# Adapter weights fetched in pieces of 512 bytes instead of 2 KB

## The reference

```
x      : (128, 32, 512) float32          ids : (128,) int32, drawn from 3..7
weight : (8, 512, 512) float32
out    = x + einsum('bsi,boi->bso', x, weight[ids])
```

## Time and profile before

| | |
|---|---|
| median of 3 runs | 113.01 us (112.57 to 115.44) |
| the profiled execution's own time | 112.28 us |
| its span, first to last instruction | 110.4 us |
| PE busy | 101.7 us, 92% |
| ACT busy, DVE busy | 56.9 us (52%), 53.4 us (48%) |
| granted TensorE clock | 1.000 throughout |
| DMA | 22.92 MB, mean 208 GB/s |

### The profile page before, as it was taken

How to read it: one execution, slowest core, us unless ns; L and a number is a source line. 1 busy time by engine, 2 the same in 40 slices (tenths; PEclk the granted TensorE clock), 3 DMA queues, 4 the chain that set the end, 5 groups by cost and what they waited for, 6 DMA issues and landing times.

```text
span 110.4 us, 2351 instructions
## 1 busy us (share of the span) xinstructions
PE 101.7 (92%) x458; PEld 81.6 (74%) x458; DVE 53.4 (48%) x107; ACT 56.9 (52%) x103; POOL 36.1 (33%) x45
## 2 busy tenths in 40 slices
PE   5399995998999999999999999999999999999960
PEld 3148883875888888888888888888888888888840
DVE  1286952794844483468663575556282222220000
ACT  3108404567932892399575749738494443442220
POOL 7200000024670257036653624531634334330000
PEclk9999999999999999999999999999999999999999
DMA  1815597898899699947776476675466564723333
GB/s 21 290 70 144 145 384 188 265 296 214 283 353 375 142 292 365 364 135 229 254 228 216 135 255 186 220 221 183 127 198 225 186 239 130 233 116 110 101 95 95
DMA packets 25598, 22.92 MB, mean 208 GB/s; under 512 B 3264, under 2 KB 20672, under 8 KB 25584
## 3 DMA queue, kind: packets, MB, share of 16 engines
q1 hardware_dynamic: 20112, 9.84, 32.2%
q0 software_dynamic: 2400, 7.54, 18.1%
q10 hardware_dynamic: 3072, 5.37, 15.8%
HBM read 17.30 MB, written 8.91 MB: 238 GB/s over the span
## 4 chain that ended last, share of the span: by engine, by line
PE 72%; DMA 7%; ACT 5%; SPq 4%; DVE 4%; issue 3%; ACTq 1%; DVEq 0%
PE out_ps L461 72%; DMA x_raw<-in_x 4%; DMA ids_i<-in_ids 3%; SPq L158 3%; ACT w_hi L283 2%; ACT xt_hi L268 2%; DVE w_raw L375 1%; SPq L152 1%; ACT out_tile L290 1%; DVE w_lo L379 1%; DVE xt_lo L384 0%; ACTq L264 0%; DVE masked L355 0%; DVE in_slot L361 0%; DVE is_own L346 0%
## 5 line engine op out<-in xcount | busy, mean ns | idle before, releaser
L461 PE MATMUL out_ps<-w_hi,xt_hi 128*128 x136 | 53.4, 393 | 1.7 <-ACT xt_hi L268 1.7
L243 POOL DMA_INDIRECT out<-out_tile,row_of x30 | 33.3, 1111 | 61.2 <-ACT out_tile L290 57.9
L461 PE MATMUL out_ps<-w_lo,xt_hi 128*128 x136 | 53.0, 390 | 0.0
L384 DVE TENSOR_TENSOR xt_lo<-x_raw,xt_hi 128x512 fp32r<-128x512 f32 x34 | 23.6, 694 | 33.8 <-ACT xt_hi L268 33.7
L461 PE MATMUL out_ps<-w_hi,xt_lo 128*128 x136 | 36.4, 389 | 0.0
L268 ACT ACTIVATE xt_hi<-x_raw 128x512 fp32r<-128x512 f32 (+1 forms) x35 | 21.5, 616 | 20.8 <-DMA x_raw<-in_x 19.6
L461 PEld LDWEIGHTS out_ps<-w_hi,xt_hi 128*128 128x128 f32 x136 | 25.5, 188 | 8.2 <-issue 3.1
L461 PEld LDWEIGHTS out_ps<-w_hi,xt_lo 128*128 128x128 f32 x136 | 25.5, 188 | 5.4
L461 PEld LDWEIGHTS out_ps<-w_lo,xt_hi 128*128 128x128 f32 x136 | 25.5, 188 | 5.1
L283 ACT ACTIVATE w_hi<-w_raw 128x512 fp32r<-128x512 f32 x32 | 19.4, 621 | 15.0 <-DVE w_raw L375 15.0
L290 ACT ACTIVATE out_tile<-out_ps 128x512 f32<-128x512 f32 x34 | 19.9, 586 | 12.8 <-PE out_ps L461 12.8
(11 more groups left out here) (50 smaller groups left out, 8.8 us busy)
## 6 DMA issues: line engine op xcount, KB each, us to landing
x_raw<-in_x SPq DMA_DIRECT2D x134, 64.0 KB, 2.1
w_raw<-in_weight ACTq DMA_DIRECT2D x7, 1024.0 KB
w_raw<-in_weight ACTq DMA_DIRECT2D x2, 256.0 KB, 4.6
w_raw<-in_weight SPq DMA_DIRECT2D x2, 256.0 KB, 5.0
out<-out_tile ACTq DMA_DIRECT2D x8, 64.0 KB, 1.8
out<-out_tile SPq DMA_DIRECT2D x8, 64.0 KB, 1.8
out<-out_tile,row_of POOLq DMA_INDIRECT x30, 3.3
x_raw<-in_x ACTq DMA_DIRECT2D x2, 64.0 KB
```

The lines of the kernel that those rows point to most:

```text
L243: nc.gpsimd.indirect_dma_start(out=out_rows, out_offset=bass.IndirectOffsetOnAxis(ap=row_of[:, t:t + 1], axis=0), in_=out_tile[n][:, :], i ...
L384: nc.vector.tensor_tensor(xt_lo[t % XT_BUFS][:, :, :, :], x_raw[t % X_BUFS][:, :, :, :].rearrange("p m c r -> p c m r"), xt_hi[t % XT_BUFS ...
L461: return nc.tensor.matmul(out_ps[n][:, :], left[k][:, c, :, :].rearrange("p m r -> p (m r)"), right[:, bass.ds(rank, 1), c, :].rearrange(" ...
```

## The change

The cap on one piece of the weight DMA of ranks 1 to 7 goes from 4 * D = 2048 bytes to D = 512 bytes. A piece is one contiguous run that a DMA engine handles as a unit. The bytes, the buffers, the issuing engine, the waits and the order are the same. Rank 0's weights, x and the stores are untouched.

```
                 act.dma_start(w_raw[n][:, :, :], w_t[bass.ds(k & (KEY - 1), 1), :, :, :].rearrange("a p c o -> (a p) c o"),
-                              cond=k >= KEY if j >= W_BUFS else None, max_dma_last_dim=4 * D).then_inc(w_loaded[n], 16)
+                              cond=k >= KEY if j >= W_BUFS else None, max_dma_last_dim=D).then_inc(w_loaded[n], 16)
```

## The result

The median went from 112.88 us (runs on the same chip) to 114.60 us, a ratio of 1.0167 with a 95% interval of 1.0125 to 1.0209: 1.7 us slower by the medians, 1.9 by the ratio, outside noise and inside 2%. All ratios here compare only the executions within 1.5% of the fastest of their kernel, since single executions of the kernel before took anything from 111.9 to 115.6 us in the later batch that e1 to e3 are compared with. The profiled execution took 114.44 us, its span is 112.5 us against 110.4.

The account below looks back on a forecast made before the run. PE was taken to bound the kernel, unbroken from tile 5, with 2.6 us of holes before. Tile 2 +0.5 and tile 5 +0.3 made +0.8 us on 113.01: 113.8 us, range 111.9 to 116.4.

Parts of the forecast that it names:

- the upper price: Weight loads: case of 0.8 us more per load, giving +1.6 us in sum, 114.6 us.
- Issuing, and packets: ACT's issue: at most 0.1 us more, 0 in the sum; its queue's packets go from 3072 to 9216.
- Price of a load, "+0.5 us": Each executed weight load takes 0.5 us longer in 512-byte pieces, bounds 0 and 0.8 us.
- my upper bound: Weight load priced at 308 GB/s, 3.40 us against 2.60 at 404 GB/s: 0.8 us more a load.
- Tile 2, "+0.5": Ahead of tile 2: x behind rank 1's load comes 0.5 us later uncovered, so PE's hole grows by 0.5 us.
- a hole near 1.75 us: Sign of being right: PE's idle time ahead of tile 2 near 1.75 us, from 1.25 before.
- Tile 5, "it takes 0.5 longer; less 0.2 of slack", +0.3 more: Rank 2's load, issued 0.5 us later and 0.5 longer, less 0.2 slack, delays tile 5 by 0.8 us, 0.3 beyond tile 2.
- Tiles 9 and 13, "nothing": Loads of ranks 3 and 4: covers of 0.57 and 0.95 us ahead of these tiles absorb 0.5 us, costing nothing.
- Supply: Rival, 0.18: small pieces are made ready more slowly than engines move them; 117.1 us at half price, 122.9 at full.
- Turns: Rival, 0.17: engines alternate between queues, so x gets through earlier and tile 2's hole closes; 112.2 us, at best 110.4.
- "Doesn't do what it says": Rival, 0.15: pieces shrink only on the writing side; 113.0 to 113.5 us, packet count not reaching 9216.
- Line rate from 512 bytes on: Skill's statement on weight DMA: 512-byte transfers suffice for line rate, so no extra load cost, time stays 113.0 us.

Follow-up runs that it names:

- e1: Kernel before with only rank 1's weight load in 512-byte pieces; ratio 1.0053 to the kernel before.
- e3: Kernel before with only the loads of ranks 3 and 4 (and the skipped ones behind) in 512-byte pieces; ratio 0.9993 to the kernel before.
- e4: Separate kernel with only the weight load, five piece sizes, without and with x loads behind; alone 5.16 us in 2 KB pieces, 5.72 us in 512-byte pieces.
- e2: Kernel before with only rank 2's weight load in 512-byte pieces; ratio 1.0131 to the kernel before.
- e8: Separate kernel with one weight load among x loads, no routing or products; first pair 5.44 us in 2 KB pieces, 6.33 us in 512-byte pieces.
- e9: Only rank 2's load in 512-byte pieces, x of tile 6 and later held back until it landed; ratio 1.0503 to the kernel before.
- e7: Kernel before, 2 KB pieces, with ACT splitting tile 1 before it issues rank 1's load; ratio 1.0089 to the kernel before.
- e11: Full change (512-byte pieces) with weights of rank 2 and later prepared one round later; ratio 1.0000 to the kernel before.
- e10: Kernel before, 2 KB pieces, with weights of rank 2 and later prepared one round later; ratio 1.0024 to the kernel before.
- e6: Kernel before with the weight loads in 8 KB pieces; ratio 1.0107 to the kernel before.
- e12: Kernel before with the weight loads in 256-byte pieces; ratio 1.0339 to the kernel before.
- e5: Kernel before with the weight loads in 1 KB pieces; ratio 1.0048 to the kernel before.

## Why the prediction was right or wrong

The forecast was +0.8 us, 113.8; measured was 114.6, 1.7 us above the median of before, twice the change that was forecast. The range held it, it lay within 2%, and the mechanism is the one named; two terms were mis-sized. That 114.6 is also the sum at the upper price is in part luck: that sum had 0.8, 0.6 and 0.2 us for tiles 2, 5 and 9, and the trace has 0.83, 1.3 and 0.

*Issuing, and packets: right.* ACT spent 0.39 us on the 2048 pieces, against 0.41; 9216 packets, 17.4% of the engines, as forecast.

*Price of a load, "+0.5 us": too small.* Alone it is 0.6 us (e4); with x behind, the weights come 0.85 us later (e4), and in the kernel the last x of tile 2 took 5.11 us in place of 4.31, 0.80 more. My rows compared weights in 2 KB at 404 GB/s with x at 336, the first stretch behind the weights; with all pieces small the engines ran at 289 and 288 GB/s, and the load alone fell from 346 to 297. The stretch of 308 GB/s, my upper bound, was the nearer row.

*Tile 2, "+0.5":* +0.83 us. Same error. The sign that I gave, a hole near 1.75 us, was a bad one (0.91 measured): it took the start of tile 0 as fixed, and in the kept traces tile 0 starts anywhere from 11.1 to 12.5 us.

*Tile 5, "it takes 0.5 longer; less 0.2 of slack", +0.3 more: the step that failed in size.* From issue to `add_one` rank 2's load took 26.42 - 18.98 = 7.44 us, 1.1 more than before, and 1.4 more in e2 (0.7 to 0.9 is seen in e8, x traffic included). The tile started 1.3 us later than tile 2's shift alone would give (2.13 - 0.83). That the second load lay bare, with hardly any slack, was right, and is what made a small price large.

*Tiles 9 and 13, "nothing": right, with less cover than I said.* e3 is 0.9993, and with the full change PE ran without a hole from tile 5 on. But PE starts a tile 0.24 us after its x split ends (before, tile 5's split ended at 26.61 + 0.64 = 27.25 us and PE started it at 27.49), which I left out: the covers were 0.33 and 0.71 us, not 0.57 and 0.95, and 0.33 is less than the price. e3's longest execution lost 1 us in holes ahead of tiles 8 and 9.

*Supply: refuted.* The engines are full at every size; even in 256-byte pieces the load alone takes 6.5 us.

*Turns: half true.* One x load lands early with small pieces (e4), as it would by round robin between queues, and in e9 x and weight pieces share the late engine; the x loads that SP issues later don't come early. So the gain never reached tile 2. The Trainium skill's round robin (DMA: Bandwidth & Descriptors, Queues, rings and completion order) fits that first x load, but not the later ones of e4, which landed behind the weights in 512-byte pieces; e7, which only changed the order of issue, moved tile 2 by 1.25 us.

*"Doesn't do what it says": refuted by the packet count.*

*Line rate from 512 bytes on (the Trainium skill, same page, Specifications):* not what e4 shows; 395 GB/s in 2 KB pieces, and 346 falling to 297 GB/s in 512-byte pieces, through the middle.

**Open:** some 0.5 us of rank 2's 1.4. It is not there in the load without the rest of the kernel (e8), not caused by the x of tile 6 and later, and it sits on one late engine (e9; in e2, too, the weights' last pieces have 6.8% of 16 engines at 24.5 to 25.0 us). In before, after, e2 and e9 one instruction fetch of 16 KB, which holds an engine for about 1 us, falls into 21.5 to 24 us, on the same 16 DMA engines, and e8 has none; but before has it too, with a much shorter tail. Whether it makes one of them late was not tried. Open too are which x loads get turns, and why 8 KB pieces made the kernel slower.

## What to carry to other kernels

Size a transfer's price with the company that it has, and look for the wait that has no slack: here a load that is 0.6 to 0.9 us longer by itself cost nothing on two of four, 0.6 us on one and 1.5 us on the one whose landing and use had been at most some 0.2 us apart, an estimate. Where the use could be put one round later for nothing, the kernel no longer felt the transfer (e11), though it got no faster (e10). Compare the starts of tiles between two traces, not their holes, and look at the granted clock and at the total of the execution that was profiled before taking its trace for the typical one.

## What the runs showed of the hardware

A small x load that SP issues right behind ACT's 1 MB load can wait for nearly all of it, on another queue and on 16 shared engines: issued at 18.16 us against 18.11, it took 5.68 us (e6), where 2.1 us is the median before. In e7 one issued 0.03 us behind took 3.0. A single one of the 16 engines can hold up a whole load: in e9 one worked alone for the last microsecond. And a longer hole costs PE twice. In e11 PE idled 2.26 us ahead of tile 2; then the granted clock (third figure from the end), in stretches around it:

```profile
17.00:19.50 2.50, 0.28 (x2) 0.00 (x0) 0.17 (x1) 0.63 (x1) 0.00 (x0) 1.00 1.06 258
19.90:23.10 3.20, 3.20 (x9) 2.52 (x8) 2.00 (x4) 1.84 (x4) 0.00 (x0) 0.50 0.83 233
23.50:26.50 3.00, 3.00 (x15) 2.46 (x14) 2.21 (x4) 2.04 (x5) 0.99 (x1) 1.00 1.19 298
```

0.50 of 2.4 GHz is the lower level, 1.2 GHz; tile 2 took 4.43 us there (19.55 to 23.98) in place of 2.86. Holes of 1.98 us (e7), 2.04 (e1), 2.32 (e12) and 2.90 (e9) were followed by a granted clock of 0.50 to 0.59 over the next 3 us and more; holes of 1.25 us (before), 1.60 (e5), 1.76 (after) and 1.82 (e2) were not. Of e11's twelve executions three show a mean clock of 0.983 or 0.984 and took 114.1 to 114.3 us, eight took 112.5 to 113.2, and one 115.2 at 0.997.
